# A fused Macaron block (two mixture-of-experts FFNs around a local attention) on one core: VectorE's empty copies removed, two softmax reductions fused, and two steps moved in ScalarE's and GpSimd's programs

## The chip, the core and the metric

The kernel runs on one core of a Trainium2 chip. A core has five engines with programs of their own: TensorE (PE: matmuls; its weight loads are listed as PEld), VectorE (DVE), ScalarE (ACT), GpSimd (POOL) and SyncE (SP, here only DMA issues). They synchronise by semaphores. The metric is the device time of one execution in microseconds; the time before is the median of three runs.

## The reference

x is 4 x 2048 rows of 256 numbers. Three sublayers follow one another, each on a layer norm of x and added to x:

```python
def ffn(x):                       # E = 8 experts, the best K = 2 per row
    gates = softmax(x @ Wg + bg)
    topk_gates, topk_idx = top_k(gates, 2)
    topk_gates = topk_gates / sum(topk_gates)
    expert_out = einsum('nd,edo->neo', x, We) + be
    return sum(take(expert_out, topk_idx) * topk_gates)
def attn(x):                      # 16 heads of 16; each row sees rows s-1, s, s+1
    xp = x @ Wp.T + bp
    q, k, v = (xp @ Wq.T + bq) * scale, xp @ Wk.T + bk, xp @ Wv.T + bv
    out = softmax(q . k[s-1, s, s+1]) @ v[s-1, s, s+1]
    return out @ Wo.T + bo
x = x + 0.5 * ffn(layernorm(x))
x = x + attn(layernorm(x))
x = x + 0.5 * ffn(layernorm(x))
```

## The kernel before

The 8192 rows are 64 tiles of 128 rows, and two tiles make a pair. All three sublayers of different pairs are in flight at once: in round s (from -1 to 35, written out without loops) the first FFN works on pair s, the query/key/value products on pair s-1, the scores on pair s-2, the attention's output on s-3 and the second FFN on s-4. Rounds -1 to 3 fill this pipeline, rounds 4 to 31 are steady, rounds 32 to 35 drain it. In round 1 SyncE's queue also moves q, k, v and x of the first pair by one partition, for the last group's neighbours, in 24 small DMAs (lines 241 and 243, `moved_...`); ScalarE waits for all of them in round 3.

Every matmul is done three times on float32 split into a high and a low part: activations are transposed by TensorE (line 918, `tr_bank`), ScalarE writes the high part (`hi_step`, line 409, `T_hi`), VectorE the rest (`lo_step`, line 579, `T_lo`), and `product` (lines 889 to 891) multiplies. There are four such transposes a round: TA and TD feed the first and second FFN, TB the q/k/v products, TO the output projection (`tr_bank` line 889).

The FFN evaluates all eight experts into four PSUM banks (`ffn_bank`, two experts each). ScalarE empties banks 0 and 2 (`scale_step`, line 446, into `we_raw`), VectorE banks 1 and 3 (`chain_step`, line 656, `chain_sum`), each times the gate; TensorE may refill a bank once it is emptied. GpSimd adds the pieces (`sum_step`, lines 332, 334, 340) on a `base` (`base_step`, line 324), which is x plus the gated bias, and `chain_step` of bank 1 begins with that base.

Each engine follows an order written out by hand in its `body(s)`: what stands first in an engine's program holds up everything behind it. Three parts matter here.

- VectorE's `gate_step`, part 0: logits (593, 596), the largest eight (`max`, 599), their places (`max_index`, 603), the margin of the second to the first (605), the places as numbers (607). Then `lo_step(TO)`, then parts 1 and 2 (610 to 636), whose result TensorE transposes (line 939) and turns into the bias (955). ScalarE's `second` (414) waits for the margin and stands ahead of a copy of q and k (470).
- VectorE's `weights_step`: part 0 takes the largest of three scores (699, 701: `most`) and subtracts it (703), part 1 sums three exponentials (707, 709), takes the reciprocal (711) and multiplies (713). ScalarE's `exp_step` (487) stands between.
- `await_apart` (line 558) waits for a semaphore and then copies two numbers per partition from `minus_half` to `idle`, which nobody reads; it stands ahead of `max`, `max_index` and each `bn_aggr` (574).

## Time and profile before

| what | us |
|---|---|
| median of 3 runs (lowest to highest) | 1137.74 (1134.66 to 1139.28) |
| the profiled execution | 1135.11 |
| its span, first to last instruction | 1133.3 |
| busy: PE, PEld | 1070.8 (94%), 889.8 (79%) |
| busy: DVE, POOL, ACT | 950.8 (84%), 714.8 (63%), 518.8 (46%) |
| empty copies, line 558 | 170 of them, 85.6 busy |

All durations below are from the profiled execution; about 1.8 us of it lie outside the span. Its time is 2.6 us under the median of the three runs. An instruction's duration in the profile includes the time in which it is held up after it was started, and neighbours on one engine overlap by some hundredths of a microsecond. A busy PE is not a PE at its peak, so its waits are read from the lists of waits.

### The profile page before, as it was taken

The numbers are of one execution on the slowest core, as the hardware profiler recorded it, in microseconds if no ns is written. First come the engines' busy times: TensorE is split into PE (matmuls) and PEld (weight loads), VectorE is DVE, ScalarE is ACT, GpSimd is POOL, SyncE is SP. The second block draws the span as 40 slices with busy tenths as digits, with TensorE's granted clock in tenths as the row PEclk, the third lists the DMA queues.
The fourth block names the chain that finished last, engine by engine and source line by source line (L and its number), as shares of the span: only waits on it lengthen the run. The fifth ranks groups of instructions, "written<-read, shape, count | busy, mean of one in ns | idle before, by whom it ended". The sixth has DMA issues, their size and how long they took to land.

```text
span 1133.3 us, 17965 instructions
## 1 busy us (share of the span) xinstructions
PE 1070.8 (94%) x5459; PEld 889.8 (79%) x5459; DVE 950.8 (84%) x2675; ACT 518.8 (46%) x1181; POOL 714.8 (63%) x953
## 2 busy tenths in 40 slices
PE   4898799999999999999999999999999999998785
PEld 2676688888888888888888888888888888887563
DVE  3659789898898898888888989888889898988873
ACT  3253454444455544544555444445554444444331
POOL 2465466666676666666766676667666766563443
PEclk9899899999999999999999999999999999999988
DMA  5001000000000000000000000000000000000000
GB/s 162 10 30 35 12 15 6 19 20 20 19 19 20 14 6 19 20 19 20 20 19 11 10 19 20 19 20 19 20 12 8 19 20 20 10 10 10 10 10 19
DMA packets 12583, 23.05 MB, mean 20 GB/s; under 512 B 2212, under 2 KB 5812, under 8 KB 12488
## 3 DMA queue, kind: packets, MB, share of 16 engines
q1 hardware_dynamic: 9240, 13.37, 3.4%
q0 software_dynamic: 3248, 8.54, 2.7%
q8 instruction: 44, 0.72, 0.3%
q14 instruction: 51, 0.42, 0.1%
HBM read 12.47 MB, written 8.39 MB: 18 GB/s over the span
## 4 chain that ended last, share of the span: by engine, by line
PE 80%; DVE 9%; SPq 3%; DMA 2%; issue 2%; ACT 2%; POOL 1%; DVEq 0%; POOLq 0%; ACTq 0%
PE ffn_bank L889 18%; PE ffn_bank L891 18%; PE ffn_bank L890 18%; PE tr_bank L918 5%; PE tr_bank L930 4%; PE mix_bank L890 3%; PE mix_bank L891 3%; PE mix_bank L889 3%; SPq L243 2%; PE tr_bank L889 2%; DVE chain_sum L656 2%; PE mix_bank L955 1%; DMA we_raw<-in_L_ffn_We 1%; PE tr_bank L891 1%; PE tr_bank L890 1%
## 5 line engine op out<-in xcount | busy, mean ns | idle before, releaser
L889 PE MATMUL ffn_bank<-we_hi,T_hi 128*128 128x512 f32 x1024 | 416.3, 407 | 3.8 <-DVE chain_sum L656 2.5
L891 PE MATMUL ffn_bank<-we_hi,T_lo 128*128 128x512 f32 x1024 | 404.9, 395 | 0.0
L890 PE MATMUL ffn_bank<-we_lo,T_hi 128*128 128x512 f32 x1024 | 404.0, 395 | 0.0
L332 POOL TENSOR_TENSOR chain_sum<-chain_sum,we_raw 128x512 f32<-128x512 f32 x128 | 165.8, 1295 | 184.4 <-DVE chain_sum L656 184.4
L446 ACT ACTIVATE we_raw<-ffn_bank,gate 128x256 f32<-128x256 f32 x512 | 208.1, 479 | 134.7 <-PE ffn_bank L891 134.6
L889 PEld LDWEIGHTS ffn_bank<-we_hi,T_hi 128*128 128x128 f32 x1024 | 195.3, 191 | 46.1 <-issue 4.6
L891 PEld LDWEIGHTS ffn_bank<-we_hi,T_lo 128*128 128x128 f32 x1024 | 194.5, 190 | 43.2
L890 PEld LDWEIGHTS ffn_bank<-we_lo,T_hi 128*128 128x128 f32 x1024 | 195.6, 191 | 35.5
L409 ACT CAST T_hi<-tr_bank 128x512 fp32r<-128x512 f32 x128 | 75.0, 588 | 121.8 <-PE tr_bank L918 121.6
L656 DVE SCALAR_TENSOR_TENSOR chain_sum<-ffn_bank,gate,base 128x256 f32<-128x256 f32 x128 | 61.4, 479 | 77.2 <-POOL base L324 49.3
L656 DVE SCALAR_TENSOR_TENSOR chain_sum<-ffn_bank,gate,chain_sum 128x256 f32<-128x256 f32 x256 | 110.7, 473 | 8.4 <-PE ffn_bank L891 8.4
L334 POOL TENSOR_TENSOR pool_sum<-chain_sum,we_raw 128x256 f32<-128x256 f32 x128 | 108.4, 847 | 10.0
L309 POOL TENSOR_TENSOR var_eps<-mean_var,eps 128x2 f32<-128x2 f32 x96 | 20.7, 216 | 144.1 <-DVE mean_var L574 144.1
L579 DVE TENSOR_TENSOR T_lo<-tr_bank,T_hi 128x512 fp32r<-128x512 f32 x128 | 87.0, 682 | 27.6 <-ACT T_hi L409 27.6
L889 PE MATMUL mix_bank<-wqkv_hi,T_hi 128*128 128x512 f32 (+1 forms) x256 | 90.1, 352 | 5.0 <-ACT qk L470 5.0
L558 DVE COPY idle<-minus_half 128x2 f32<-128x2 f32 x170 | 85.6, 504 | 5.9
L891 PE MATMUL mix_bank<-wqkv_hi,T_lo 128*128 128x512 f32 (+1 forms) x256 | 87.9, 343 | 0.0
L890 PE MATMUL mix_bank<-wqkv_lo,T_hi 128*128 128x512 f32 (+1 forms) x256 | 87.8, 343 | 0.0
L383 POOL DMA_INDIRECT x_in<-in_L_attn_x,x_row x60 | 66.9, 1115 | 18.2 <-issue 9.1
L312 POOL TENSOR_TENSOR rstd<-var_eps,minus_half 128x2 f32<-128x2 f32 x96 | 77.0, 802 | 0.0
L429 ACT ACTIVATE normed<-x,shift,rstd 128x256 f32<-128x256 f32 x128 | 70.6, 609 | 6.4 <-POOL shift L314 6.3
L918 PE MATMUL tr_bank<-ident,normed 128*128 128x128 f32 x384 | 59.9, 281 | 8.0 <-ACT normed L429 7.9
(128 smaller groups left out, 1862.2 us busy)
## 6 DMA issues: line engine op xcount, KB each, us to landing
out_x<-y SPq DMA_DIRECT2D x31, 256.0 KB, 2.0
we_raw<-in_L_ffn_We SPq DMA_DIRECT2D x2, 1024.0 KB, 13.9
x_in<-in_L_attn_x,x_row POOLq DMA_INDIRECT x60, 2.9
x_in<-in_L_attn_x SPq DMA_DIRECT2D x2, 256.0 KB, 7.5
moved_qk<-qk SPq DMA_DIRECT2D x4, 124.0 KB
w_raw<-in_L_attn_Wq SPq DMA_DIRECT2D x1, 256.0 KB, 2.8
w_raw<-in_L_attn_Wk SPq DMA_DIRECT2D x1, 256.0 KB, 3.0
w_raw<-in_L_attn_Wv SPq DMA_DIRECT2D x1, 256.0 KB, 3.9
```

Of the source, the lines that this page charges most:

```text
L312: nc.gpsimd.tensor_tensor(rstd[:, ln], var_eps[:, ln], minus_half[:], ALU.pow).then_inc(done, 1)
L332: nc.gpsimd.tensor_tensor(chain_sum[:, f, t], chain_sum[:, f, t], scaled[:, f, t, 1], ALU.add).then_inc(done, 1)
L334: nc.gpsimd.tensor_tensor(pool_sum[:, f, t], chain_sum[:, f, t, 0], scaled[:, f, t, 0, 1], ALU.add).then_inc(done, 1)
L409: nc.scalar.copy(halves(i, n)[0][:].rearrange("p t k n -> p (t k n)"), t_bank[i][:, :]).then_inc(hi_done[i], 1)
L446: last = nc.scalar.activation(scaled[:, f, t, half, j], ffn_bank[b][:, j * D:(j + 1) * D], ACT.Copy, scale=gate[:, 2 * f + t, e:e + 1])
L558: nc.vector.tensor_copy(idle[:], minus_half[:])
L579: nc.vector.tensor_tensor(lo[:].rearrange("p t k n -> p (t k n)"), t_bank[i][:, :], hi[:].rearrange("p t k n -> p (t k n)").bitcast(f32), ...
L656: nc.vector.scalar_tensor_tensor(out=chain_sum[:, f, t, j], in0=ffn_bank[b][:, j * D:(j + 1) * D], scalar=gate[:, 2 * f + t, e:e + 1], in1 ...
L889: nc.tensor.matmul(dest, hi[:, t, k, :], w_hi_[:, k, c0:c1], start=(first and k == 0), stop=False, skip_group_check=not first)
L890: nc.tensor.matmul(dest, hi[:, t, k, :], w_lo_[:, k, c0:c1], start=False, stop=False, skip_group_check=not first)
L891: last = nc.tensor.matmul(dest, lo[:, t, k, :], w_hi_[:, k, c0:c1], start=False, stop=(k == KB - 1), skip_group_check=not first)
L918: last = nc.tensor.transpose(t_bank[i][:, at:at + PART], source[:, t, k * PART:(k + 1) * PART], ident[:])
```

## The change

It does four things. Every `await_apart` becomes a plain wait on the instruction behind it, and `idle` goes. In `gate_step` the margin moves ahead of the four `max_index`. In `weights_step` the two `max` become one `tensor_reduce` over the three scores, and the two additions one `tensor_reduce` as well. In the orders by hand, GpSimd's `base_step(FFN1, s + 1)` moves ahead of the two `sum_step(FFN2, s - 4, ...)`, and ScalarE's `hi_step(TD, s - 3)` ahead of `exp_step(s - 2)`.

```diff
@@ gpsimd, body
+                if (s + 1).within(PAIRS):
+                    base_step(FFN1, s + 1)
                 if (s - 4).within(GROUPS):
                     sum_step(FFN2, s - 4, 0)
                     sum_step(FFN2, s - 4, 1)
-                if (s + 1).within(PAIRS):
-                    base_step(FFN1, s + 1)
@@ scalar, second_step
-                act.wait_ge(gate_ops, g.times(GATE_OPS, 5))
+                act.wait_ge(gate_ops, g.times(GATE_OPS, 4))
@@ scalar, body
+                if (s - 3).within(GROUPS):
+                    hi_step(TD, s - 3)
                 if (s - 2).within(GROUPS):
                     exp_step(s - 2)
-                if (s - 3).within(GROUPS):
-                    hi_step(TD, s - 3)
@@ vector, stats_step
-                await_apart(stat_done[ln], n.times(4, 2))
+                dve.wait_ge(stat_done[ln], n.times(4, 2))
@@ vector, gate_step, part 0
-                    await_apart(ops, g.times(GATE_OPS, 2))
+                    after(2)
                     for c in range(cs.start, cs.stop):
                         last = nc.vector.max(top[:, c], logits[:, c])
                     last.then_inc(ops, 1)
-                    await_apart(ops, g.times(GATE_OPS, 3))
+                    after(3)
+                    nc.vector.tensor_tensor(margin[:, cs], top[:, cs, 1], top[:, cs, 0], ALU.subtract).then_inc(ops, 1)
                     for c in range(cs.start, cs.stop):
                         last = nc.vector.max_index(top_at[:, c], top[:, c], logits[:, c])
                     last.then_inc(ops, 1)
-                    nc.vector.tensor_tensor(margin[:, cs], top[:, cs, 1], top[:, cs, 0], ALU.subtract).then_inc(ops, 1)
-                    after(4)
+                    after(5)
                     nc.vector.tensor_copy(top_no[:, cs], top_at[:, cs, 0:2]).then_inc(ops, 1)
@@ vector, weights_step
-                    nc.vector.tensor_tensor(most[:, 0], score[:, 0], score[:, 1], ALU.max).then_inc(ops, 1)
-                    after(5)
-                    nc.vector.tensor_tensor(most[:, 1], most[:, 0], score[:, 2], ALU.max).then_inc(ops, 1)
+                    nc.vector.tensor_reduce(most[:], score[:].rearrange("p m h -> p h m"), AX.X, ALU.max).then_inc(ops, 2)
...
-                    nc.vector.tensor_tensor(total[:, 0], prob[:, 0], prob[:, 1], ALU.add).then_inc(ops, 1)
-                    after(8)
-                    nc.vector.tensor_tensor(total[:, 1], total[:, 0], prob[:, 2], ALU.add).then_inc(ops, 1)
+                    nc.vector.tensor_reduce(total[:, 0], prob[:].rearrange("p m h -> p h m"), AX.X, ALU.add).then_inc(ops, 2)
```

VectorE in a late steady round, from the logits to the low part of TO. Before (names end in the buffer's number only where it matters, `x` is x1, x2):

```order
L593 TENSOR_TENSOR logits<-tr_bank,bg_all 128x32
L596 TENSOR_TENSOR logits<-tr_bank,logits 128x32
L558 COPY idle<-minus_half 128x2
L599 MAX top<-logits 128x8 x4
L558 COPY idle<-minus_half 128x2
L603 MAX_INDEX top_at<-top,logits 128x8 x4
L605 TENSOR_TENSOR margin<-top 128x4
L607 CAST top_no<-top_at 128x8
L579 TENSOR_TENSOR T_lo_0<-tr_bank,T_hi_0 128x512
```

and now:

```order
L587 TENSOR_TENSOR logits<-tr_bank,bg_all 128x32
L590 TENSOR_TENSOR logits<-tr_bank,logits 128x32
L593 MAX top<-logits 128x8 x4
L596 TENSOR_TENSOR margin<-top 128x4
L598 MAX_INDEX top_at<-top,logits 128x8 x4
L601 CAST top_no<-top_at 128x8
L573 TENSOR_TENSOR T_lo_0<-tr_bank,T_hi_0 128x512
```

Both copies are gone, and the margin stands in front of the four `max_index`.

VectorE in the same round, from the second FFN's bank 3 past the low part of TD. Before:

```order
L656 SCALAR_TENSOR_TENSOR chain_sum<-ffn_bank,gate,chain_sum 128x256 x2
L699 TENSOR_TENSOR most<-score 128x32
L701 TENSOR_TENSOR most<-most,score 128x32
L703 TENSOR_TENSOR score<-score,most 128x96
L579 TENSOR_TENSOR T_lo_1<-tr_bank,T_hi_1 128x512
L656 SCALAR_TENSOR_TENSOR chain_sum<-ffn_bank,gate,base 128x256
```

and now:

```order
L650 SCALAR_TENSOR_TENSOR chain_sum<-ffn_bank,gate,chain_sum 128x256 x2
L693 TENSOR_REDUCE most<-score 128x32
L695 TENSOR_TENSOR score<-score,most 128x96
L573 TENSOR_TENSOR T_lo_1<-tr_bank,T_hi_1 128x512
L650 SCALAR_TENSOR_TENSOR chain_sum<-ffn_bank,gate,base 128x256
```

One reduction stands for the two `max`.

GpSimd in a steady round, from the last norm to the gathers of x. Before:

```order
L314 TENSOR_TENSOR shift<-minus_mean,rstd 128x2
L332 TENSOR_TENSOR chain_sum<-chain_sum,we_raw 128x512
L334 TENSOR_TENSOR pool_sum<-chain_sum,we_raw 128x256
L340 TENSOR_TENSOR y<-pool_sum,chain_sum 128x256
L332 TENSOR_TENSOR chain_sum<-chain_sum,we_raw 128x512
L334 TENSOR_TENSOR pool_sum<-chain_sum,we_raw 128x256
L340 TENSOR_TENSOR y<-pool_sum,chain_sum 128x256
L324 TENSOR_TENSOR base<-x_in,bias_sum 128x512
L383 DMA x_in<-in_L_attn_x,x_row 128x256 x2
```

and now:

```order
L313 TENSOR_TENSOR shift<-minus_mean,rstd 128x2
L323 TENSOR_TENSOR base<-x_in,bias_sum 128x512
L331 TENSOR_TENSOR chain_sum<-chain_sum,we_raw 128x512
L333 TENSOR_TENSOR pool_sum<-chain_sum,we_raw 128x256
L339 TENSOR_TENSOR y<-pool_sum,chain_sum 128x256
L331 TENSOR_TENSOR chain_sum<-chain_sum,we_raw 128x512
L333 TENSOR_TENSOR pool_sum<-chain_sum,we_raw 128x256
L339 TENSOR_TENSOR y<-pool_sum,chain_sum 128x256
L382 DMA x_in<-in_L_attn_x,x_row 128x256 x2
```

The base of the next pair (`base<-x_in,bias_sum`) went from behind the six sums of the second FFN to ahead of them.

## Rows read from the trace of the kernel before

**Rows 1.** The page: shares of the chain that ended last; the empty copy's group (busy, mean ns | idle before).
```profile
PE 80%; DVE 9%; SPq 3%; DMA 2%; issue 2%; ACT 2%; POOL 1%; DVEq 0%; POOLq 0%; ACTq 0%
...
L558 DVE COPY idle<-minus_half 128x2 f32<-128x2 f32 x170 | 85.6, 504 | 5.9
```

**Rows 2.** Stretches, us and busy (x count) of PE, PEld, DVE, ACT, POOL; PEclk, DMA, GB/s.
```profile
148.00:990.00 842.00, 840.81 (x4397) 705.99 (x4397) 750.73 (x2089) 409.94 (x937) 579.06 (x752) 1.00 0.05 17
...
1042.30:1045.30 3.00, 3.00 (x9) 2.33 (x8) 2.18 (x11) 0.83 (x3) 1.05 (x2) 0.50 0.23 87
```

**Rows 3.** Waits from 148 to 990 us (waiting <- waited for: us in total, times, longest us).
```profile
PEld tr_bank L889 <- DVE T_lo L579: 2.2, 12, 0.2
...
PE ffn_bank L889 <- ACT we_raw L446: 1.0, 3, 0.6
```

**Rows 4.** Waits from 990 us to the end, TensorE's weight loads.
```profile
PEld tr_bank L889 <- DVE T_lo L579: 6.1, 3, 2.8
...
PEld ffn_bank L889 <- DVE chain_sum L656: 4.0, 4, 1.9
...
PEld tr_bank L918 <- issue: 3.3, 1, 3.3
PEld tr_bank L930 <- DVE T_lo L579: 3.0, 2, 1.8
```

**Rows 5.** VectorE in a steady round (start us, us, engine, line, operation).
```profile
532.77 1.04 DVE L558 COPY idle<-minus_half 128x2 f32<-128x2 f32 x1
...
535.43 0.68 DVE L579 TENSOR_TENSOR T_lo<-tr_bank,T_hi 128x512 fp32r<-128x512 f32 x1
```

**Rows 6.** GpSimd beside it.
```profile
532.50 1.29 POOL L332 TENSOR_TENSOR chain_sum<-chain_sum,we_raw 128x512 f32<-128x512 f32 x1 [1.06 <-DVE chain_sum L656]
```

**Rows 7.** VectorE in the drain.
```profile
1058.54 1.29 DVE L701 TENSOR_TENSOR most<-most,score 128x32 f32<-128x32 f32 x1
1059.86 0.26 DVE L703 TENSOR_TENSOR score<-score,most 128x96 f32<-128x96 f32 x1
...
1068.08 1.08 DVE L558 COPY idle<-minus_half 128x2 f32<-128x2 f32 x1
...
1070.75 0.68 DVE L579 TENSOR_TENSOR T_lo<-tr_bank,T_hi 128x512 fp32r<-128x512 f32 x1
...
1083.12 0.84 DVE L703 TENSOR_TENSOR score<-score,most 128x96 f32<-128x96 f32 x1
```

**Rows 8.** GpSimd in the drain.
```profile
1058.48 1.29 POOL L332 TENSOR_TENSOR chain_sum<-chain_sum,we_raw 128x512 f32<-128x512 f32 x1 [1.23 <-DVE chain_sum L656]
...
1069.21 0.72 POOL L334 TENSOR_TENSOR pool_sum<-chain_sum,we_raw 128x256 f32<-128x256 f32 x1
```

**Rows 9.** ScalarE in the drain.
```profile
1060.34 0.57 ACT L409 CAST T_hi<-tr_bank 128x512 fp32r<-128x512 f32 x1
```

**Rows 10.** The fill: two steps of the chain that ended last (start, us, what).
```profile
70.16 0.48 ACT qk L470
...
105.67 10.64 DMA moved_x_bo<-x_bo
```

**Rows 11.** TensorE ahead of the first of them.
```profile
69.26 0.39 PE L891 MATMUL mix_bank<-wqkv_hi,T_lo 128*128 128x512 f32 x1
```

**Rows 12.** A gate step without other work on TensorE: GpSimd's last sum and VectorE's fourth instruction after it.
```profile
51.36 0.73 POOL L340 TENSOR_TENSOR x<-pool_sum,chain_sum 128x256 f32<-128x256 f32 x1
...
52.22 0.19 DVE L610 TENSOR_TENSOR hot<-expert_no,top_no 128x32 f32<-128x32 f32 x1
```

**Rows 13.** One line's durations, min/median/max ns: the two reductions that are there now.
```profile
L751 DVE TENSOR_REDUCE row_mask<-ident x8: 157/158/169, 1.5 to 2.0; 128x1 f32<-128x16 f32 x8
...
L688 DVE TENSOR_REDUCE score<-prod x32: 1733/1740/1753, 95.6 to 1079.2; 128x96 f32<-128x1536 f32 x32
```

**Rows 14.** All waits of the run: VectorE for GpSimd's base.
```profile
DVE chain_sum L656 <- POOL base L324: 49.3, 28, 2.0
```

14 lines of the change are left out of this document (5 added, 9 removed).

## The prediction

> **What bounds the kernel now.** I read the page first, then the stretches, then who waited for whom, and only then the timelines. The chain that ended last is TensorE's for 80% [rows 1]. In the steady rounds TensorE is busy for 840.8 of 842 us at the upper of its two clock levels, 2.4 GHz (granted 1.00), while VectorE is busy for 750.7 [rows 2]. So an instruction less on VectorE is worth nothing there by itself; only what TensorE waits for counts, and the lists of waits say how much that is. From 148 to 990 us it waits 2.2 us in 12 rounds for VectorE's T_lo (of the TO transpose) and 1.0 us for ScalarE to empty a bank [rows 3]. From 990 us on, in the drain, there are fewer matmuls to hide VectorE behind, and TensorE waits 6.1 and 3.0 us for T_lo, 4.0 us for VectorE's bank sums and 3.3 us before the TO transpose, which the list puts down to "issue" and which ends with T_lo of TB [rows 4]: 16.4 us. These two lists, 3.2 and 16.4 us, and the fill are all that the change can take from.
>
> **What a copy costs.** The 170 copies are 85.6 us busy, 504 ns each [rows 1]; for two numbers that is waiting. The pattern is in the timelines: the copy that starts at 532.77 ends at 533.81, and GpSimd's sum that started at 532.50 ends at 533.79 [rows 5, 6]. It is the same with the maximum at 1058.54 (ends 1059.83), beside a sum from 1058.48 to 1059.77 [rows 7, 8]. VectorE's instruction is held until GpSimd's ends. The two reductions of the trace have no such tail: over the run their durations stay within 157 to 169 and 1733 to 1753 ns [rows 13].
> The Trainium skill (SBUF — State Buffer, section "Who interferes with whom") states that VectorE and GpSimd share a port pair, held for a whole instruction; a VectorE instruction with two SBUF inputs, or a copy or cast in a 2-port mode, contends for it, and `tensor_reduce` never does on trn2. The trace agrees, by the rows just named. It speaks against the change's bookkeeping: the wait is not removed with the copy, the next two-input instruction behind it takes it over.
> So the gain is never 504 ns each. What counts at each place is what stands between GpSimd's end and the result that somebody needs.
>
> **Gate step, up to T_lo of TO (the steady wait, and the drain).** In the drain the logits are ready at 1068.08; copy, `max`, second copy, `max_index`, margin follow, and T_lo starts at 1070.75, 2.67 us later [rows 7]. Now: two `max` at once, the margin (two SBUF inputs) held until GpSimd's first sum ends, at 1069.13 (it started 0.08 before GpSimd's second, at 1069.21), then `max_index` to about 1069.4, then the cast to `top_no`. Whether that cast is held by the second sum, until 1069.93 [rows 8], no row shows, since none of the 37 fell beside one; the copy is its nearest relative and was held, so I take held: T_lo starts at 1069.87, 0.88 us earlier. Not held it would be 1.2. In a steady round the same sequence ends with T_lo at 535.43 + 0.68, 3.34 us after the first copy's start [rows 5], with TensorE 0.2 us ahead of it; any of these gains covers that. The 2.2 us go, and with them, by ScalarE's new order (below), the 1.0: **3.2 us in the steady rounds**. Zero would mean that another wait takes their place.
>
> **Softmax.** The maximum at 1058.54 and its predecessor become one reduction of 96 numbers. The rows bound it between 0.16 (16 numbers) and 1.74 us (1536); by the slope between them, 1.04 ns a number, it is 0.24 [rows 13]. It is not held, but the subtraction behind it is, until 1059.77; it then ends at about 1059.9 instead of 1060.12 [rows 7, 8]: 0.2 us. At 1083.12 the subtraction was held a second time, 0.84 instead of 0.26 [rows 7]; there 0.8 us go. In the second half two additions of 32 numbers become one such reduction. Not held, each is a little shorter than the unheld subtraction of 96 numbers, 0.26 us [rows 7]; I take 0.2 each, so 0.16 us are saved.
>
> **ScalarE's order.** T_hi of TD (0.57 us) stood behind the exponential, and so behind VectorE's subtraction, at 1060.34, although its transposes had long been done [rows 9]. Now it lies in the idle time before, and the bank scaling behind the exponential starts 0.57 us earlier. VectorE's T_lo of TD starts right after its subtraction, about 1 us earlier, and TensorE's logits wait for it: the 3.0 us of two such waits [rows 4]. Should the transposes come later than the subtraction, the exponential would now wait for them, by up to the 0.57 us it gained. The row has no wait of its own in brackets, so there they were done in time; I price that at nothing.
>
> **GpSimd's order.** VectorE waited 49.3 us in 28 rounds for the base, at most 2.0 at a time, since it stood behind six sums [rows 14]. It now comes ahead of them and VectorE runs up to 2 us ahead. In steady rounds TensorE does not wait for what follows, so this is hidden by TensorE; it is worth something once, where the drain begins and VectorE is behind. There the next thing that is late is the projection, TensorE's own, so I take 0.9 of the 2.0 us. The six sums come later by the base's length, 1.3 us (a GpSimd sum of as many numbers, [rows 6]); behind them are the store of y and the scaling of the next round, neither of which shows among TensorE's waits.
>
> **The other copies** (before `bn_aggr`) lie beside TensorE's bank products. Held they cost 0.5 us like the rest, otherwise far less; no wait of TensorE hangs on the statistics in the lists, and I take nothing. The gathers on GpSimd's queue move up with the work before them.
>
> **The sum in the drain**, wait by wait:
> - begin of the drain, T_lo of TO: 0.3
> - TO transpose (the wait of 3.1): 0.9 from the base, 0.2 and 0.16 from the softmax, 0.57 from T_hi: 1.8
> - next round: 0.2 + 0.57 + 0.16 = 0.9 up to the TO transpose, then 0.9 at T_lo
> - next round: 0.8 + 0.57 + 0.16 = 1.5, then 0.9
> - last gate step: there TensorE waits for the whole gate. GpSimd's last sum ends at 52.09 in the like place of the fill, and the instruction `hot` at 52.41 [rows 12]; now `hot` itself is what is held until 52.09, so 0.3.
> That is **6.6 of the 16.4 us**. The 4.0 us for the bank sums stay, since they hang on the projection and the score products, which nothing here shortens.
>
> **Fill.** The same 0.3 at the gate step of round 0. In round 1 the copy of q and k stood behind the margin and started at 70.16, while TensorE had finished at 69.65 [rows 10, 11]: 0.4. With it start the 24 moves, whose last lands at 116.31 and releases TensorE [rows 10]. **0.7 us.**
>
> **Total: 3.2 + 6.6 + 0.7 = 10.5 us.** The profiled execution (1135.1) would become 1124.6, its span 1122.8; it lay 2.6 us under the median of three, so against the median 1137.7 - 10.5 = **1127.2 us**.
>
> **Rivals.**
> - *The next wait takes over.* What VectorE gives earlier is then awaited from elsewhere: after T_lo of TO come the projection, x2, the score products and the bank sums, all still one behind another. For: 4.0 us of waits for bank sums remain and each of the four is up to 1.9 us long [rows 4]. Against: T_lo, logits and TO transposes are the longest waits and directly behind the shortened parts. With the steady 2.2 and a third of the rest (2.4) the gain is 4.6: 1133.
> - *More than the sum.* The cast is not held (0.3 at two places), and low-clock work disappears. After the wait of 3.1 us before the TO transpose, the granted clock was 0.50 at 1042.3 to 1045.3, that is 1.2 GHz [rows 2]. At the upper level the work of these 3 us takes half as long; a shortened wait may spare the 1.5. With three of them and the cast: 1122.
> - *Slower: the clock.* The same row read the other way. The waits change their lengths and places, and with them the places at which the granted clock falls to 1.2 GHz. Each new stretch like this one costs 1.5 us. To end over 0.5% slower they must eat the 10.5 and 5.7 more: 16 us, eleven such stretches, more than the drain has room for beside its waits. It decides only from the point where it reaches into the steady rounds, whose clock is 1.00 now: one stretch in every third of them. Time then: 1144 and more.
> - *It doesn't do what it says.* The wait now on `max`, `max_index` and `bn_aggr` may cost an instruction of its own. No row shows one; at the 0.16 us of VectorE's shortest instructions [rows 13] the some 20 of them in the drain give back 3 us: 1130, inside my range and counted with the first rival.
>
> **Chances.** Forecast 0.64, next wait takes over 0.24, more than the sum 0.08, slower by the clock or something unseen 0.04. A measurement of this kernel tells about 0.5%, 5.7 us, from no change (three runs lay 4.6 us apart): faster by that means under 1132.1, which holds for the forecast, the better case and a small part of the first rival: faster 0.73, same 0.23, slower 0.04. The range: from the better case less the scatter, 1121, to the first rival, 1134.
>
> **What would show it.** T_lo of TO starting under 2 us after the last logits in the drain; no wait of TensorE for T_lo of TO in the steady rounds, and no bank wait; VectorE's wait for the base near zero; the subtraction, not the maximum, with the long duration; VectorE's busy time down by some 100 us with nothing to show for most of it; the moves starting 0.7 us earlier. It is wrong if the 26 rounds of the steady stretch take longer than today's 32.4 us on average, or if TensorE's waits in the drain stay near 16 us under another name.

## The result, and the profile after

The changed kernel takes **1119.2 us** (median of 6 runs, 1119.0 to 1121.3) where before, beside it, takes 1136.6 (6 runs, 1133.9 to 1139.5): ratio 0.985, 95% interval 0.983 to 0.987. The gain is 17.4 us; the prediction had 10.5 and a range from 1121 to 1134. Repeated beside the last experiments (e16), the same change gave 0.986 (0.984 to 0.988).

Executions of one kernel differ, and a trace holds a single one. Before took between 1132 and 1142 us, and both of its traces (1135.1 here; 1134.6 in e1, the lowest of ten) are of executions below the median; the change took 1119 to 1121. So a difference between two traces can lie some us beside that of the medians.

The page after, the shares of the chain that ended last (before: 80% and 9% [rows 1]):

```profile
PE 85%; DVE 6%; SPq 3%; DMA 2%; issue 1%; ACT 1%; POOL 0%; POOLq 0%; DVEq 0%; ACTq 0%
```

The stretch from the gate's transpose of round 4 to that of the last full round (26 rounds), and the five rounds of the drain (us, busy of PE, PEld, DVE, ACT, POOL, granted clock, DMA, GB/s), after:

```profile
146.67:983.45 836.78, 836.78 (x4396) 700.64 (x4395) 704.37 (x1911) 419.56 (x936) 578.23 (x753) 1.00 0.05 17
983.45:1096.50 113.05, 100.42 (x505) 80.20 (x504) 94.90 (x245) 45.78 (x106) 57.14 (x72) 1.00 0.03 12
```

and the same drain of before:

```profile
990.68:1112.43 121.75, 105.66 (x504) 84.90 (x503) 101.92 (x274) 44.97 (x106) 58.55 (x74) 0.94 0.03 12
```

TensorE's waits in the drain after (before: [rows 4]), and the largest of VectorE in the steady rounds, where the base of [rows 14] stood:

```profile
PEld ffn_bank L879 <- DVE chain_sum L650: 4.2, 3, 1.9
PEld tr_bank L908 <- DVE attn L726: 4.1, 2, 2.1
PEld tr_bank L879 <- DVE T_lo L573: 3.9, 2, 2.0
PEld tr_bank L908 <- issue: 2.2, 1, 2.2
```

```profile
DVE chain_sum L650 <- PE ffn_bank L881: 59.0, 88, 1.3
```

The profiled span fell from 1133.3 to 1117.5 us. Measured from one transpose of the gate to the next, the last one starts 15.9 us earlier (1096.5, was 1112.4), and that splits so: the fill ends 2.1 us earlier (146.7, was 148.8), the 26 steady rounds take 5.1 us less (836.8 against 841.9), the drain 8.7 us less (113.05 against 121.75). Predicted were 0.7, 3.2 and 6.6. In the drain TensorE's idle time (stretch less busy) fell from 16.1 to 12.6 us, 3.5; the other 5.2 are busy time, and the granted clock there rose from 0.94 to 1.00. The second traces of the two kernels (e1 and e16) agree within 0.2 us in the steady rounds and 0.4 in the drain, but only within 0.7 in the fill.

### The profile page after: what moved, and what is told of

The parts are those of the page before. It is cut to its first block, busy times and chain, and to the rows that moved or that the text cites. A ratio compares the mean times of both kernels' runs of the same rounds, so it can differ in the third digit from the quotient of the medians.

```text
span 1117.5 us, 17795 instructions
## 1 busy us (share of the span) xinstructions
PE 1062.5 (95%) x5459; PEld 879.8 (79%) x5459; DVE 893.1 (80%) x2441; ACT 529.5 (47%) x1181; POOL 713.3 (64%) x953
## 4 chain that ended last, share of the span: by engine, by line
PE 85%; DVE 6%; SPq 3%; DMA 2%; issue 1%; ACT 1%; POOL 0%; POOLq 0%; DVEq 0%; ACTq 0%
PE ffn_bank L879 20%; PE ffn_bank L880 19%; PE ffn_bank L881 19%; PE tr_bank L908 5%; PE tr_bank L920 4%; PE mix_bank L879 4%; PE mix_bank L881 4%; PE mix_bank L880 4%; SPq L242 2%; PE mix_bank L945 2%; PE tr_bank L879 1%; PE tr_bank L881 1%; PE tr_bank L880 1%; DMA we_raw<-in_L_ffn_We 1%; DMA moved_x_bo<-x_bo 1%
## 5 line engine op out<-in xcount | busy, mean ns | idle before, releaser
L308 POOL TENSOR_TENSOR var_eps<-mean_var,eps 128x2 f32<-128x2 f32 x96 | 28.8, 300 | 136.5 <-DVE mean_var L568 136.5
L333 POOL TENSOR_TENSOR pool_sum<-chain_sum,we_raw 128x256 f32<-128x256 f32 x128 | 104.2, 814 | 10.0
L323 POOL TENSOR_TENSOR base<-x,bias_sum 128x512 f32<-128x512 f32 x32 | 42.1, 1317 | 68.9 <-issue 59.9
L382 POOL DMA_INDIRECT x_in<-in_L_attn_x,x_row x60 | 66.3, 1105 | 15.3 <-issue 13.3
L908 PEld LDWEIGHTS tr_bank<-ident,normed 128*128 128x128 f32 x384 | 46.3, 143 | 25.3 <-ACT normed L428 17.0
```

The costliest lines, as they stand in the source:

```text
L333: nc.gpsimd.tensor_tensor(pool_sum[:, f, t], chain_sum[:, f, t, 0], scaled[:, f, t, 0, 1], ALU.add).then_inc(done, 1)
L908: last = nc.tensor.transpose(t_bank[i][:, at:at + PART], source[:, t, k * PART:(k + 1) * PART], ident[:])
```

## The experiments

Each kernel below was profiled and timed beside before, whose median was 1139.0 us beside e1 to e4, 1135.7 beside e5 to e8, 1136.4 beside e9 to e12 and 1136.5 beside e13 to e16; the ratio is to that. "Steady" is the 26 rounds, "drain" the five behind them, "clock" the granted clock in the drain, "distance" the mean time in ns from the start of one FFN matmul of 512 columns to the start of the next, all from the profiled run (a difference of 0.1 ns means nothing). "Old places" means that every tile has its address of before.

| kernel | time | ratio (95%) | fill ends | steady | drain | clock | distance |
|---|---|---|---|---|---|---|---|
| before | 1136.6 | 1 | 148.8 | 841.9 | 121.8 | 0.94 | 228.6 |
| the change | 1119.2 | 0.985 (0.983-0.987) | 146.7 | 836.8 | 113.1 | 1.00 | 233.1 |
| e1 before again | 1140.8 | 1.001 (1.000-1.003) | 148.3 | 842.1 | 121.4 | 0.96 | 228.8 |
| e16 the change again | 1120.0 | 0.986 (0.984-0.988) | 147.4 | 837.0 | 113.0 | 1.00 | 233.2 |
| e2 change, old places | 1115.0 | 0.979 (0.977-0.980) | 148.3 | 830.2 | 114.3 | 0.99 | 228.6 |
| e3 before, new places | 1137.7 | 0.998 (0.996-0.999) | 147.3 | 845.6 | 122.7 | 0.96 | 233.2 |
| e4 all copies out | 1120.1 | 0.983 (0.981-0.985) | 148.5 | 832.5 | 116.5 | 0.99 | 228.6 |
| e8 gate's copies out | 1119.9 | 0.986 (0.984-0.987) | 148.8 | 832.3 | 115.7 | 0.99 | 228.6 |
| e7 reductions | 1125.4 | 0.991 (0.989-0.993) | 148.4 | 834.9 | 119.2 | 0.97 | 228.8 |
| e6 both orders | 1121.8 | 0.987 (0.985-0.990) | 148.0 | 829.9 | 120.7 | 0.93 | 228.5 |
| e13 base's order | 1134.5 | 0.999 (0.997-1.000) | 149.5 | 848.4 | 118.9 | 0.97 | 228.5 |
| e15 T_hi's order | 1120.7 | 0.986 (0.983-0.989) | 149.1 | 831.3 | 118.6 | 0.97 | 228.8 |
| e9 change less orders, old places | 1117.1 | 0.983 (0.981-0.985) | 149.2 | 830.5 | 114.3 | 1.00 | 228.6 |
| e10 change with copies, old places | 1114.6 | 0.982 (0.979-0.984) | 147.9 | 827.8 | 115.9 | 0.97 | 228.7 |
| e11 T tiles 8 bytes up | 1115.0 | 0.981 (0.979-0.983) | 148.2 | 830.3 | 114.3 | 0.99 | 228.6 |
| e12 T tiles 32 bytes up | 1113.3 | 0.980 (0.978-0.981) | 147.2 | 829.4 | 114.2 | 0.99 | 228.8 |
| e5 old places up to T_lo | 1115.1 | 0.982 (0.980-0.984) | 147.4 | 830.5 | 114.3 | 0.99 | 228.7 |
| e14 e12 with the copies before bn_aggr | 1111.6 | 0.979 (0.977-0.981) | 147.0 | 827.0 | 114.3 | 0.99 | 228.7 |

### First: is the gain the copies, and do the tiles' places matter?

Before again, unchanged, as a yardstick. Its trace confirms the expectation: 228.8 ns, and a steady stretch within 0.2 us of the first.

> The kernel before, unchanged, profiled a second time beside the others of this call. In its first profile the 512-column matmuls of the FFN banks followed each other at 228 to 229 ns in every round, in the changed kernel's at 233 ns. If that is a matter of the chip or the moment, this profile shows about 233 ns here or the others show 228; if it belongs to the program, 228 to 229 again. It also tells how much the steady rounds of one and the same kernel differ: I expect the three rounds with a wait of 0.3 to 0.6 us for a bank at other places or in another number, within 2 us in total.

The change removes the tile `idle` (8 bytes) and shrinks two others, so that nearly every tile moves. e2 is the change at the old places:

```
+        idle = sb("idle", [PART, 2])            # unused, at its old place
         most = sb("most", [PART, 2 * H])
+        spare = sb("spare", [PART, 2 * H])
         total = sb("total", [PART, 2, 2 * H])
+        spare2 = sb("spare2", [PART, 2 * H])
```

> The changed kernel with the tile idle (8 bytes a partition) allocated again where it was, never written, and the two tiles of the softmax padded to their old sizes, so that every tile has its old address; no instruction differs. Theory 'addresses': taking 8 bytes out ahead of T_hi and T_lo is what raised the distance of the 512-column matmuls from 228 to 233 ns; then this kernel is back at 228, which is worth up to 5 ns x 3300 matmuls = 16 us, so 1105 to 1112 us. Theory 'order': the distance comes from the order of the work or from elsewhere; then the time is the changed kernel's, 1119.

e3 is before with `idle` allocated last, so that the tiles behind it lie 8 bytes lower:

```
-        idle = sb("idle", [PART, 2])
         ...
         y = sb("y", [PART, 2, 2, D])
+        idle = sb("idle", [PART, 2])
```

> The kernel before with the same copies, but the tile idle allocated last, so that everything from minus_half on lies 8 bytes lower, as in the changed kernel. Theory 'addresses': 233 ns between the matmuls instead of 228 and a slower kernel, by up to 16 us, 1145 to 1152. Theory 'order': no difference, within 0.3% of before.

e4 is before without the copy's line and nothing else:

```
             def await_apart(s, value):
                 dve.wait_ge(s, value)
-                nc.vector.tensor_copy(idle[:], minus_half[:])
```

> Only the empty copies are taken out, their waits stay on the instructions behind them; order, margin and softmax are as before, and idle stays allocated. My prediction gives this part little by itself: in the gate step max and the max_index run at once, and the margin is held by GpSimd's sums in the copies' place; T_lo of TO then comes 0.9 to 1.2 us earlier, which takes the steady wait (2.2 us) and 0.9 at three places of the drain, with 0.7 in the fill: 5 to 6 us, 1131. The rival, that this part is nearly the whole change, would be 1122 or less; that the waits only pass on, 1136.

Two surprises. The copies alone give 18.9 us by the medians (14.9 between the traces), nearly the whole, where I had expected 5 to 6; and the change at its old places is 4.2 us faster than as given (3.7 between the traces). With the new places, and only then, the FFN matmuls are 233 ns apart instead of 229, in e3 as in the change. So the theory "addresses" holds for the distance, but its sizes were too large: e2 was to take 1112 us or less, and e3 was to become slower than before. In e3 the longer distances cost 10.2 us of the steady rounds, and 5.6 of them come back at the two places of the projection in the table below, because a later TensorE no longer has to wait for T_lo there. Over 300 to 900 us TensorE does fewer matmuls although it is busy in all of it (after, and e12 below, whose T tiles lie elsewhere; the number in brackets behind PE is the count):

```profile
300.00:900.00 600.00, 600.00 (x3162) 502.82 (x3161) 505.20 (x1381) 301.26 (x673) 415.37 (x543) 1.00 0.05 17
```

```profile
300.00:900.00 600.00, 599.39 (x3182) 508.38 (x3182) 505.44 (x1392) 303.91 (x680) 425.61 (x548) 1.00 0.05 17
```

### Second: which part?

e6 moves both steps and does nothing else:

```
+                base_step(FFN1, s + 1)          # GpSimd: ahead of the FFN2 sums
                 sum_step(FFN2, s - 4, 0)
                 sum_step(FFN2, s - 4, 1)
-                base_step(FFN1, s + 1)
 ...
+                hi_step(TD, s - 3)              # ScalarE: ahead of the exponential
                 exp_step(s - 2)
-                hi_step(TD, s - 3)
```

> Before with the two moved steps alone: GpSimd's base of FFN1 ahead of the FFN2 sums, ScalarE's T_hi of TD ahead of the exponential. Copies, softmax, margin and all addresses as before. My prediction had 0.9 us for the base and 0.57 for T_hi in each of three rounds of the drain, some 2.3 in all, and the bank waits of the steady rounds, 1.0: 1136. Rival: the copies are what makes each part late, and with them in place the order brings nothing: within 1 us of before. Second rival: the order also frees VectorE early in rounds 31 and 32, where taking out the copies alone brought nothing (31.44 and 28.32 us against 31.47 and 28.12): then these two rounds fall to about 30.5 and 27, and the time is near 1137 less 2 in these rounds alone.

e7 has the two reductions of the softmax alone (the hunk of weights_step in the diff, with `spare` and `spare2` kept):

> Before with the two reductions of the softmax alone (the halves that are no longer needed stay allocated, so that no address moves). My prediction had 0.36 us in the first round of the drain in which it counts and 0.36 and 0.96 in the next two, 1.7 in all, nothing in the steady rounds: 1137.3 where before has 1139. Rival: the reduction over a stride is dearer than the two instructions in its place, and the time is 1139 or more. Second rival: two instructions less per round leave VectorE earlier in the steady rounds as taking out the copies did, and the steady stretch (842.1 us) falls by 1 us or more.

e8 takes out only the two copies of the gate step:

```
-                    await_apart(ops, g.times(GATE_OPS, 2))
+                    after(2)
 ...
-                    await_apart(ops, g.times(GATE_OPS, 3))
+                    after(3)
```

> Before with the two copies of the gate step out, those before max and max_index; the copies before bn_aggr stay, as do all addresses. Taking out all copies brought 18.9 us: 9.6 in the steady rounds and the rest in the drain. Theory A, that of the prediction: only the gate step's copies stand between a result and a wait of TensorE (T_lo of TO), so this alone brings nearly all of it: the steady stretch 832.5, the time 1121. Theory B: what counts is how far VectorE is behind in all, and the copies before bn_aggr are the larger number (some 96 of 170): then this brings under half, 1131 and more. A result near 1126 would say that both count.

For e6 and e7 the expected times were far too long (1136 and 1137.3 us); only the second rival of e7 had named the steady rounds, and that of e6 two rounds of the drain, which did fall (30.5 and 27.4 us). Theory A of e8, drawn from e4's result, came out (832.5 and 1121 expected). Against before, the orders alone take 12.0 us off the steady stretch and 1.1 off the drain, the reductions 7.0 and 2.6, the gate's copies 9.6 and 6.1: 38.4 us in sum, while the change at the old places has 11.7 and 7.4, 19.1 us. The parts don't add up, because they pay in large part for the same thing. (The margin's move was not tried by itself.)

**What they pay for.** The list of waits shows 3.2 us for the steady rounds [rows 3], yet 12 can be had there. TensorE's instructions overlap in the profile, and so hide a short wait. TensorE in before, around the projection's first matmul and around the gate's transpose (start, duration; no row has an idle time in brackets):

```profile
535.88 0.28 PE L891 MATMUL mix_bank<-wqkv_hi,T_lo 128*128 128x256 f32 x1
536.16 0.39 PE L889 MATMUL tr_bank<-wo_hi,T_hi 128*128 128x256 f32 x1
536.38 0.28 PE L890 MATMUL tr_bank<-wo_lo,T_hi 128*128 128x256 f32 x1
...
537.58 0.28 PE L891 MATMUL tr_bank<-wo_hi,T_lo 128*128 128x256 f32 x1
537.76 0.33 PE L939 MATMUL tr_bank<-ident,gate_parts 128*128 128x128 f32 x1
537.86 0.47 PE L889 MATMUL ffn_bank<-we_hi,T_hi 128*128 128x512 f32 x1
```

and VectorE's last instruction of the gate beside it; T_lo of [rows 5], started at 535.43, ends at 536.11:

```profile
537.48 0.23 DVE L636 TENSOR_TENSOR gate_parts<-gate,gate_parts 128x64 f32<-128x64 f32 x1
```

Matmuls of 256 columns follow each other every 0.12 us and last 0.28. From 535.88 to 536.16 it is 0.28: the projection's first matmul, ahead of which TensorE's program waits for T_lo, started 0.05 us after T_lo's end, 0.16 late, and 535.88 + 0.28 covers the gap. The one behind it came 0.22 later instead of 0.12. The same happens at the transpose of the gate (0.18; gate_parts ended at 537.71) and behind it (0.10 to the next). In the change nothing of this is left; T_lo starts at 529.09, and the matmuls are even:

```profile
529.09 0.67 DVE L573 TENSOR_TENSOR T_lo<-tr_bank,T_hi 128x512 fp32r<-128x512 f32 x1
...
531.14 0.23 DVE L630 TENSOR_TENSOR gate_parts<-gate,gate_parts 128x64 f32<-128x64 f32 x1
```

```profile
531.37 0.28 PE L881 MATMUL mix_bank<-wqkv_hi,T_lo 128*128 128x256 f32 x1
531.48 0.28 PE L879 MATMUL tr_bank<-wo_hi,T_hi 128*128 128x256 f32 x1
...
532.77 0.28 PE L881 MATMUL tr_bank<-wo_hi,T_lo 128*128 128x256 f32 x1
532.88 0.28 PE L929 MATMUL tr_bank<-ident,gate_parts 128*128 128x128 f32 x1
532.92 0.47 PE L879 MATMUL ffn_bank<-we_hi,T_hi 128*128 128x512 f32 x1
```

There is a fifth place. The second of the three transposes of `normed` in a round is followed by an FFN matmul into a bank that ScalarE must have emptied:

```profile
549.95 0.60 PE L918 MATMUL tr_bank<-ident,normed 128*128 128x128 f32 x4
550.48 0.47 PE L889 MATMUL ffn_bank<-we_hi,T_hi 128*128 128x512 f32 x1
```

```profile
549.50 1.57 ACT L446 ACTIVATE we_raw<-ffn_bank,gate 128x256 f32<-128x256 f32 x4
```

The second of these four scalings ends at 550.34, the matmul starts 0.14 us later, and it is 0.14 to 0.15 in each of the 26 rounds. The last of the four transposes started at 550.27, and with nothing to wait for, as in e2, the matmul comes 0.03 behind that.

Summed over the 26 rounds, the time from one start to the next at these five places, worked out from the starts in the traces, in us:

| from, to | before | e7 | e8 | e6 | e2 |
|---|---|---|---|---|---|
| last qk/v matmul, first of the projection | 5.84 | 4.50 | 3.12 | 3.12 | 3.12 |
| 104 pairs of a first and a second projection matmul | 15.12 | 14.45 | 12.48 | 12.48 | 12.48 |
| last of the projection, transpose of the gate | 5.02 | 5.03 | 3.19 | 3.19 | 3.19 |
| transpose of the gate, first FFN matmul | 2.54 | 2.54 | 0.67 | 0.67 | 0.67 |
| second transpose of `normed`, FFN matmul | 6.58 | 1.47 | 5.61 | 3.43 | 0.74 |

The first four give 9.1 us in e6 and e8, all of what can be had there; the fifth gives 3.2 in e6 and 1.0 in e8. Together that is the 12.0 and the 9.6 us, within 0.4. In e2 the five give 14.9 us, and 3.3 are lost again ahead of the transposes of `normed` (see the fifth part). In e7 it is the other way round: 5.1 of its 7.0 us come from the fifth place, since with its shorter softmax the exponential, and with it the scalings, starts earlier (on average 10.9 instead of 11.2 us after the gate's transpose), and 2.0 from the projection. What the first four places ask for is small. In before T_lo ends 0.17 us after the start of the last qk/v matmul (mean of the 26 rounds), where 0.12 is the usual distance. e8 and e6 end it 1.4 and 1.6 us earlier, far more than needed, e7 only 0.08. Once VectorE is ahead, more brings nothing at these four.

### Third: take one part away from the whole

e9 is e2 with both steps at their old places in the order. e10 is e2 with all 170 copies put back:

> The change on the addresses of before (1115.0 where before has 1139.0, ratio 0.979) with the two moved steps undone: GpSimd's base of FFN1 is again behind the FFN2 sums, T_hi of TD behind the exponential; copies out, reductions and margin as in the change. So far each part alone brought more than half of the whole: orders alone 0.9874, gate copies 0.9856, softmax 0.9908. Theory (a common floor): in the steady rounds TensorE started the projection and the transpose of the gate just when VectorE was done, and every part that gives VectorE 0.3 us per round removes that; beyond, nothing is gained. Then without the orders the steady stretch stays within 3 us of 830.2, and only rounds 31 and 32 (30.5 and 27.1 us) go back towards 31.4 and 28.3: 1117.5, ratio 0.981. Rival (the orders are what counts, since alone they brought the steady stretch to 829.9): the steady stretch goes back to 835 and the time to 1122.

> The same kernel with the empty copies put back, both those of the gate step and those before bn_aggr; orders, reductions and margin as in the change, addresses of before. Theory of the common floor: the steady stretch stays at 830 and the copies cost only in the drain, where VectorE is late; taking out all of them alone brought 5.2 us in the five rounds of the drain, the other parts shorten the same waits: 1117.5, ratio 0.981. Rival (the copies are what counts, as the 18.9 us of taking them out alone suggest): 1125 or more.

Both stay at 1117 and 1115, with 830.5 and 827.8 us in the steady rounds, as the theory of a common floor had it, so neither part is needed there. The copies are all there again in e10, busy for 75.7 us (85.6 in [rows 1]), and the kernel is as fast as e11 beside it, which has none (1114.6 and 1115.0); it loses 1.6 us in the drain and gains 2.4 in the steady rounds:

```profile
L560 DVE COPY idle<-minus_half 128x2 f32<-128x2 f32 x170 | 75.7, 446 | 5.9
```

e13 and e15 split the two moves of e6. This was the open question: neither showed as a wait of TensorE in the steady rounds.

> Before with one moved step: GpSimd's base of FFN1 ahead of the FFN2 sums. Theory A: it is this one that frees the steady rounds. VectorE waited 49.3 us for the base, and TensorE started the projection and the transpose of the gate the moment that VectorE was done; with VectorE up to 2 us ahead this ends: steady stretch 830 to 831 (before 841.9, both orders 829.9), drain nearly as before (121), time 1123, ratio 0.988. Theory B: the base alone only moves VectorE's wait to another place (T_hi of TD behind the exponential): steady stretch 838 and more, ratio 0.995.

> Before with the other moved step: ScalarE's T_hi of TD ahead of the exponential. Theory A: VectorE waits 27.6 us in 32 rounds for ScalarE's T_hi (that of the TO transpose, after the gate step's beginning), but the base wait stands ahead of it and is untouched; VectorE stays late at the projection. Steady stretch 840 to 842, drain 1 us shorter, ratio 0.998. Theory B: 0.57 us less between the exponential and what follows is as good as the 0.3 us that the gate copies gave: steady stretch 833 or less, ratio 0.991.

For e15 theory B comes nearest: T_hi alone gives 10.6 of the 12.0 us, 6.4 at the first four places and 4.8 at the fifth. e13 has no gain worth the name: 1134.5 us against 1136.5, ratio 0.999. Its trace is of the slowest of ten executions (1139.6; the others took 1133.1 to 1136.5), and there the steady stretch is 6.4 us *longer*; how long it was in the others no trace shows. T_hi's mechanism, from VectorE and ScalarE in before (a round's softmax, T_hi and T_lo of TD, ScalarE's bank scalings):

```profile
516.21 0.26 DVE L703 TENSOR_TENSOR score<-score,most 128x96 f32<-128x96 f32 x1
517.29 0.69 DVE L579 TENSOR_TENSOR T_lo<-tr_bank,T_hi 128x512 fp32r<-128x512 f32 x1 [0.82 <-ACT T_hi L409]
```

```profile
516.50 0.28 ACT L487 ACTIVATE prob<-score 128x96 f32<-128x96 f32 x1 [3.61 <-DVE score L703]
516.70 0.57 ACT L409 CAST T_hi<-tr_bank 128x512 fp32r<-128x512 f32 x1
517.16 1.20 ACT L446 ACTIVATE we_raw<-ffn_bank,gate 128x256 f32<-128x256 f32 x3
```

and in e15:

```profile
479.77 0.26 DVE L703 TENSOR_TENSOR score<-score,most 128x96 f32<-128x96 f32 x1
479.94 0.68 DVE L579 TENSOR_TENSOR T_lo<-tr_bank,T_hi 128x512 fp32r<-128x512 f32 x1
```

```profile
477.25 0.59 ACT L409 CAST T_hi<-tr_bank 128x512 fp32r<-128x512 f32 x1 [0.75 <-PE tr_bank L918]
480.06 0.28 ACT L487 ACTIVATE prob<-score 128x96 f32<-128x96 f32 x1 [2.22 <-DVE score L703]
480.25 1.55 ACT L446 ACTIVATE we_raw<-ffn_bank,gate 128x256 f32<-128x256 f32 x4
```

In before T_hi starts 0.20 us after the exponential, and VectorE idles 0.82 us for it. In e15 T_hi lies 2.8 us ahead of the exponential in ScalarE's idle time, T_lo starts 0.17 after the subtraction's start instead of 1.08: VectorE is 0.9 us ahead at this point, and its wait for the base in the steady rounds falls from 45.7 to 13.5 us; at T_lo of TO 0.26 us of the lead are left on average. The bank scalings start 0.19 behind the exponential's start instead of 0.66. In e13 the base pushes GpSimd's sums on, and in the worst rounds they hold three VectorE instructions one behind another:

```profile
484.26 0.73 DVE L699 TENSOR_TENSOR most<-score 128x32 f32<-128x32 f32 x1
485.02 1.21 DVE L701 TENSOR_TENSOR most<-most,score 128x32 f32<-128x32 f32 x1
486.26 0.85 DVE L703 TENSOR_TENSOR score<-score,most 128x96 f32<-128x96 f32 x1
```

```profile
483.64 1.29 POOL L324 TENSOR_TENSOR base<-x_in,bias_sum 128x512 f32<-128x512 f32 x1
484.89 1.29 POOL L332 TENSOR_TENSOR chain_sum<-chain_sum,we_raw 128x512 f32<-128x512 f32 x1
```

```profile
487.15 0.28 ACT L487 ACTIVATE prob<-score 128x96 f32<-128x96 f32 x1 [4.61 <-DVE score L703]
487.34 0.57 ACT L409 CAST T_hi<-tr_bank 128x512 fp32r<-128x512 f32 x1
487.80 1.57 ACT L446 ACTIVATE we_raw<-ffn_bank,gate 128x256 f32<-128x256 f32 x4
```

```profile
PE ffn_bank L889 <- ACT we_raw L446: 14.8, 26, 1.0
```

The first maximum takes 0.73 us here instead of 0.17, the second 1.21 (1.28 in before) and the subtraction 0.85 instead of 0.26. The subtraction is held like this in 11 of the 26 rounds, in before in one; counted from the gate's transpose of the round, the exponential then starts at 11.95 to 12.07, and at 11.36 to 11.49 in the rest, where it was 11.03 to 11.15 in all but three rounds of before. T_hi and the bank scalings come behind it, and TensorE waits 14.8 us for the scaled bank in 26 rounds, where it was 1.0 in 3 [rows 3]. From start to start, the first four places give 9.1 us in e13 as in e6, and the fifth takes 21.9 us instead of 6.6: 15.3 lost, 6.3 more in sum. So in this execution the base's move removes VectorE's wait for the base and turns it into this one. With T_hi's move beside it (e6) the exponential starts just as late, at 11.37 to 11.52, but the scalings behind it do not, and the fifth place falls to 3.4 us.

### Fourth: the places of the tiles

T_hi and T_lo are the stationary tiles of these matmuls, we_hi and we_lo the moving ones. Counted from the first tile, we_hi, T_hi and T_lo begin at 8 modulo 64 bytes in before and at 0 in the change, as we_hi and we_lo always do. e5 is the change with 8 bytes where idle lay and 56 behind T_lo; e11 and e12 leave every other tile as in the change (modulo 64) and shift T_hi and T_lo alone:

```
+        pad1 = sb("pad1", [PART, 2])      # e11: 8 bytes; e12: 8 numbers, 32 bytes
         T_hi = [[sb(f"T_hi{i}_{c}", ...
         T_lo = [[sb(f"T_lo{i}_{c}", ...
+        pad2 = sb("pad2", [PART, 14])     # e11: 56 bytes; e12: 8 numbers, 32 bytes
         logits = sb("logits", ...
```

> The change with two pads, nothing else: 8 bytes where idle lay, so that every tile up to T_hi and T_lo has its address of before, and 56 bytes behind T_lo, so that every tile from logits on (chain_sum, qk, v, the moved tiles) has the address of the change modulo 64. What was seen so far: with the addresses of the change a 512-column FFN matmul follows the last after 233.1 ns and round 3, with the 24 moves, takes 29.5 us; with those of before it is 228.6 ns and 31.2 us. Theory A: the distance goes by the place of the matmuls' stationary tiles, T_hi and T_lo, and the moves by that of qk, v and the moved tiles. Then the distance is 228.6 ns, the fill ends at 146.6, and the time is about 1.6 us below that of the change with all old addresses: 1113.4. Theory B: the distance goes by tiles that other engines read and write at the same time (chain_sum, prod, x1): 233.1 ns stay, and the time is 1119 to 1120. Theory C: both go by T_hi and T_lo or what lies before them: 228.6 ns and a slow round 3, 1115.

> The change with 8 bytes left free directly ahead of T_hi and 56 directly behind T_lo. So the stationary tiles T_hi and T_lo alone lie 8 bytes up, at 8 modulo 64 as in before; every other tile has the address of the change modulo 64, x_in, normed and we_raw ahead of them too. Theory A: the place of T_hi and T_lo alone sets the distance of the FFN matmuls: 228.6 ns, steady stretch 830.5, ratio 0.9785 or a little less. Theory B: it is the place of what lies ahead of them, which GpSimd, VectorE and ScalarE read and write beside the matmuls (we_raw above all), and the run with 8 bytes where idle lay moved those too: then 233.1 ns stay, steady stretch 836.8, ratio 0.984.

> As the run before, with 32 bytes ahead of T_hi and 32 behind T_lo: T_hi and T_lo at 32 modulo 64, all others as in the change. If theory A holds and what is dear is a stationary tile that begins at 0 modulo 64 (where the moving tiles we_hi and we_lo begin too), the distance is 228.6 ns here as well and the time that of the run before. If what is dear is 0 modulo 32, it stays at 233.1 ns: steady stretch 836.8, ratio 0.984. If theory B holds, both runs have 233.1.

Theory A holds for the distance: T_hi and T_lo alone set it, and both 8 and 32 modulo 64 give 228.6 to 228.8 ns (the steady stretch 830.3 and 829.4), 0 gives 233.1 (836.8). For matmuls of 256 columns it is the other way round: in the output projection 116.6 ns at 0 and 120.0 at 8 and 32. A steady round has 96 matmuls of 512 columns for the FFNs and 24 of 256 in all, so the longer distance weighs more. For one stretch of matmuls without anything between, after and before (14 intervals in 3.27 us, 11 in 2.52):

```profile
514.85 0.40 PE L879 MATMUL ffn_bank<-we_hi,T_hi 128*128 128x512 f32 x1
...
518.12 0.40 PE L881 MATMUL ffn_bank<-we_hi,T_lo 128*128 128x512 f32 x1
```

```profile
514.84 0.40 PE L889 MATMUL ffn_bank<-we_hi,T_hi 128*128 128x512 f32 x1
...
517.36 0.39 PE L891 MATMUL ffn_bank<-we_hi,T_lo 128*128 128x512 f32 x1
```

Theory A of e5 had a second half, that the 24 moves go by the places of the tiles that they move. It fell: the fill ended at 147.4 instead of 146.6, and e5's ratio (0.982) isn't below e2's (0.979). Round 3, which holds the 24 moves, takes 29.4 to 29.6 us in the three kernels with all of the new places (the change, e16, e3) and 30.4 to 32.8 in the rest; e5 has 30.4, e11 30.7, e12 31.6. What sets it stays open.

### Fifth: put together

e14 is e12 with the copies before bn_aggr back. e10's steady stretch had been 2.4 us shorter than e2's although it does more, and the place is the transpose behind `normed` (from the FFN matmul to such a transpose it is 22.5 us in sum in e2 and 19.9 in e10, 19.2 in before):

```profile
473.96 0.19 POOL L316 TENSOR_TENSOR shift<-minus_mean,rstd 128x2 f32<-128x2 f32 x1
```

```profile
472.24 0.20 POOL L316 TENSOR_TENSOR shift<-minus_mean,rstd 128x2 f32<-128x2 f32 x1
```

The first row is e2's, the other e10's. Counted from the gate's transpose of their round (467.62 and 466.30), GpSimd's `shift` starts at 6.34 in e2 and 5.94 in e10, `normed` at 6.57 and 6.36, and TensorE's transpose at 7.72 and 7.52; in e2 that is so in every second round.

> The change with the empty copies before bn_aggr put back (those of the gate step stay out) and with 32 bytes ahead of T_hi and 32 behind T_lo. Theory A: in the odd rounds of the change VectorE, now early, begins a score product just ahead of GpSimd's shift of LN1 (6.34 instead of 5.93 us after the gate's transpose), and ScalarE's normed and TensorE's transpose come 0.2 us late; the copies delay VectorE past that. Then the steady stretch is 827 to 828 as with all copies in, the drain 114.3 as without those of the gate step, the time about 1.6 us under that of the same layout without them (1113.3, ratio 0.9796): 1111.5, ratio 0.978. Theory B: the gate step's copies made that delay, not those before bn_aggr: steady stretch 829.4 to 830.3, time 1113.5 or more.

> The change as given, beside the other three on the same chip. Ratio 0.985 as before (0.983 to 0.987), profile with a steady stretch of 836.8 us and 233.1 ns between FFN matmuls of 512 columns. The version above should be 0.7% faster than it; if they differ by under 0.3%, the tile addresses matter less than the traces say.

Theory A again: steady 827.0, drain 114.3, 1111.6 us, 0.75% under the change beside it (1120.0). It has the shortest time of this study, though its ratio, 0.979, can't be told from those of e2 and e12 (0.979 and 0.980). That the copies are worth something rests on two pairs of traces, 827.8 against 830.2 and 827.0 against 829.4 us in the steady rounds. My reading is that VectorE, a little later with the copies, stays out of the way of GpSimd's statistics; that isn't shown, nor what they collide over without them.

## Why the prediction was too small

- **A copy isn't worth its 504 ns: right.** e10 has all 170 and is no slower. The wait did move to the next two-input instruction: the change's margin takes 0.79 us at 1057.02 in the drain, and the cast to `top_no` 0.49 at 1058.13 (short ones: 0.16), so the cast was held, as I took it to be: GpSimd's second sum runs from 1057.86 to 1058.59, the cast ends at 1058.62. T_lo started 1.82 us after the last logits' end, 0.85 less than the 2.67 of before (forecast 0.88). The Trainium skill (SBUF — State Buffer, section "Who interferes with whom") names casts among the instructions that can contend with GpSimd; the trace agrees, by the 0.49 us of this one. VectorE's busy time fell by 57.7 us, not the 100 I named, for the same reason.

```profile
1056.54 0.17 DVE L590 TENSOR_TENSOR logits<-tr_bank,logits 128x16 f32<-128x16 f32 x1
...
1057.02 0.79 DVE L596 TENSOR_TENSOR margin<-top 128x2 f32<-128x2 f32 x1
...
1058.13 0.49 DVE L601 CAST top_no<-top_at 128x4 f32<-128x4 uint32 x1
1058.53 0.68 DVE L573 TENSOR_TENSOR T_lo<-tr_bank,T_hi 128x512 fp32r<-128x512 f32 x1
```

- **Steady rounds, 3.2 us: the step that failed.** I read "busy 840.8 of 842" [rows 2] and concluded that "only what TensorE waits for counts, and the lists of waits say how much that is". They list idle time, and a wait shorter than the overlap of two matmuls (0.28 us long, one every 0.12: 0.16 us) is none. I had taken that overlap for some hundredths of a microsecond, as on the other engines. At equal tile places the steady rounds gave 11.7 us, nearly four times the term. My own row had the hint: T_lo ended at 536.11 [rows 5], and I called TensorE "0.2 us ahead of it" without asking when the next matmul started, 536.16.
- **Not in the prediction at all: the tiles' places.** They cost the steady rounds 6.5 us (836.8 against 830.2) and gave back 1.6 in the fill and 1.3 in the drain. That the kernel as given gained only 5.1 us in its steady rounds, not far from my 3.2, is luck: the 11.7 and the 6.5, neither of which I saw, leave 5.2. At the old places the last transpose of the gate starts 19.6 us earlier than in before, where the change has 15.9 and the forecast was 10.5.
- **ScalarE's order: right mechanism, wrong place.** 0.57 us in three rounds of the drain were forecast; alone (e15) it gave 10.6 us in the steady rounds and 3.1 in the drain. **GpSimd's order**: nothing in the steady rounds and 0.9 us in the drain were forecast. Alone (e13) it gave 2.0 us by the medians, so the size fits, but not the reason: "hidden by TensorE" leaves out the 9.1 us gained at four places and the loss at the fifth (15.3 us in the traced execution). I had looked for what waits behind the six sums on GpSimd, and not at which VectorE instructions the moved sums would then hold.
- **Copies before bn_aggr: nothing forecast.** By the traces they are worth less than nothing here (e10, e14).
- **Drain, 6.6 us: the size came out near, 8.7, but it isn't the sum that I wrote down.** The waits gave 3.5: T_lo of TO 6.1 to 3.9, the 3.3 before the TO transpose (my sum calls it 3.1) to 2.2, the logits' T_lo 3.0 to none, as forecast in direction. The wait for `attn` is 4.1 where it was 2.2, that for the bank sums 4.2 where it was 3.7; but the unchanged kernel has 3.8 and 4.0 in its second trace (e1), so this is no sign of my first rival, the next wait takes over. The other 5.2 us are busy time at a higher granted clock: before has four stretches at 0.50 in the drain (one in [rows 2]), the change none up to 1097. My rival "more than the sum", to which I gave 0.08, had named them. What such a stretch is worth in time isn't shown, and it can be less than its 1.5 us of busy time. The drain of e1, with three of them:

```profile
990.35:1111.74 121.39, 104.10 (x504) 83.72 (x503) 101.38 (x274) 45.05 (x106) 58.71 (x74) 0.96 0.03 12
```

  It is 1.6 us less busy than before's and only 0.4 us shorter; the waits took the rest. The stretches go with the long waits for T_lo of TO: all kernels in which the longest of these is 2.6 to 2.8 us (before, e1, e3, e6, e7, e10, e13, e15) have a granted clock of 0.93 to 0.97 in the drain, all in which it is 2.0 or less (the change, e2, e4, e5, e8, e9, e11, e12, e14, e16) 0.99 or 1.00, though the wait before the TO transpose is 2.9 to 3.4 us in e4, e8 and e9, as in before. That a shorter wait is the cause was not tried by itself.
- **Fill, 0.7 us: measured 2.1** in this pair of traces and 0.9 in the second (148.3 in e1, 147.4 in e16). Round 3 is 2.0 us shorter in both: the last of the moves' transfers landed at 113.7 instead of 116.3. It comes with the new places (e3 has it too), not with VectorE.
- The rival "slower: the clock" did not occur, nor did a wait on `max` cost an instruction of its own: `max` starts 0.21 us after the second logits instruction's start, as the instructions around it do.

## What to carry to other kernels

When an engine is busy all the time, don't read its slack from the list of waits: look at the distances from start to start at the places where it needs another engine's result, and see whether that result ends just before. If it does, each of several small edits may release most of it, so their gains must not be added, and the cheapest one may be enough (here one moved cast: 16 us). Take a second trace of the kernel that you compare with, and look where the traced execution lies among the others, before you read a few microseconds out of one. Before an operation is moved ahead on GpSimd, look which VectorE instructions then run beside the sums behind it; and when an edit removes a tile, keep the other tiles' addresses, or measure the new ones by themselves.

## What the hardware showed that I had not expected

- The place of the stationary tiles modulo 64 bytes changes the pace of float32r matmuls: 233.1 ns from start to start at 0, 228.6 at 8, 228.8 at 32 (512 columns, moving tiles at 0), 2% of the FFN's matmul time. At 256 columns it is 116.6 at 0 and 120.0 at 8 and 32. Other places were not tried.
- After a wait too short to be seen as idle time the next matmul comes late too: 0.22 us instead of 0.12 in the projection, 0.10 instead of 0.03 behind the gate's transpose. In the round shown a matmul 0.16 us late costs 0.26; over the 26 rounds the two together cost 0.21 us each time.
- One stretch at half the granted clock fewer in the drain, in two traces of the same kernel, took 1.6 us off TensorE's busy time and 0.4 us off the drain.
